# Retention's values: headed products in pairs of row tiles, and the first chunk's turned rows between the second chunk's pairs

## The reference

```python
V = jnp.einsum('bshd,hde->bshe', vh, Wh)
masked = scores * Dn[None, :, :, :]
A = jnp.maximum(jnp.abs(masked.sum(axis=0)), 1.0)
O = jnp.einsum('hst,bthe->bshe', A, V).reshape(b, s, dim)
mu = O.mean(axis=-1, keepdims=True)
var = O.var(axis=-1, keepdims=True)
Y = (O - mu) / jnp.sqrt(var + GN_EPS) * gn_gamma + gn_beta
W = jax.nn.relu(x @ wg_w)
return W * Y @ wo_w
```

## Time and profile before

| | |
|---|---|
| median of 3 runs | 1602.47 us (1602.07 to 1602.49) |
| the profiled execution's own time | 1602.21 us |
| its span in the profile | 1600.5 us |
| mean granted TensorE clock | 0.995 of full speed |
| TensorE (PE) busy | 1557.8 us, 97% of the span |
| VectorE (DVE) busy | 1192.6 us, 75% |
| ScalarE (ACT) busy | 1034.2 us, 65% |
| GpSimd (POOL) busy | 481.6 us, 30% |

### The profile page before, as it was taken

How to read it: one execution, slowest core, us unless ns; L and a number is a source line. 1 busy time by engine, 2 the same in 40 slices (tenths; PEclk the granted TensorE clock), 3 DMA queues, 4 the chain that set the end, 5 groups by cost and what they waited for, 6 DMA issues and landing times.

```text
span 1600.5 us, 28360 instructions
## 1 busy us (share of the span) xinstructions
PE 1557.8 (97%) x9554; PEld 1210.9 (76%) x9554; DVE 1192.6 (75%) x2455; ACT 1034.2 (65%) x2863; POOL 481.6 (30%) x516
## 2 busy tenths in 40 slices
PE   7989979999999999999999999999999999999998
PEld 6888756666776777777777777777777777777887
DVE  7668876766996888888888887777777777898322
ACT  4564437663568888778787787777777777874100
POOL 1000222224534434434334334334344344320000
PEclk9999989999999999999999999999999999999999
DMA  8631568986663232373333363121151221100001
GB/s 310 211 105 60 180 216 276 310 289 196 212 210 132 80 124 87 113 253 103 113 120 115 113 221 93 54 72 57 56 204 55 73 90 52 59 28 7 27 33 40
DMA packets 79849, 206.11 MB, mean 129 GB/s; under 512 B 7344, under 2 KB 27824, under 8 KB 74224
## 3 DMA queue, kind: packets, MB, share of 16 engines
q1 hardware_dynamic: 74048, 185.94, 34.0%
q0 software_dynamic: 5680, 18.62, 3.8%
HBM read 151.83 MB, written 52.69 MB: 128 GB/s over the span
## 4 chain that ended last, share of the span: by engine, by line
PE 79%; DVE 4%; ACT 1%; DMA 1%; POOL 1%; issue 1%; SPq 0%; POOLq 0%; ACTq 0%; DVEq 0%
PE bank L103 11%; PE bank L105 10%; PE bank L104 10%; PE bank L2682 10%; PE bank L2683 10%; PE bank L2744 7%; PE bank L2768 6%; PE bank L2733 5%; PE bank L1537 4%; PE bank L2754 3%; PE bank L1496 1%; DMA s_rows<-x_rows,t_tok 1%; POOL t_rs L2647 1%; ACT t_sc L2899 1%; PE bank L1526 1%
## 5 line engine op out<-in xcount | busy, mean ns | idle before, releaser
L2682 PE MATMUL bank<-t_half,t_xh 128*128 128x256 f16 (+1 forms) x1024 | 309.3, 326 | 0.0
L2683 PE MATMUL bank<-t_half,t_xh 128*128 128x256 f16 (+1 forms) x1024 | 306.0, 326 | 0.0
L2644 POOL TENSOR_SCALAR t_ve<-t_ss 128x4 f32<-128x4 f32 (+1 forms) x128 | 25.9, 202 | 563.8 <-DVE t_ss L2997 537.6
L2899 ACT ACTIVATE t_sc<-bank,t_mx 128x128 f32<-128x128 f32 x512 | 180.3, 381 | 15.9 <-DVE t_mx L3037 10.8
L2647 POOL TENSOR_TENSOR t_rs<-t_ve,t_mhalf 128x4 f32<-128x4 f32 (+1 forms) x128 | 172.3, 1346 | 10.7
L3001 DVE TENSOR_TENSOR t_hn<-bank,t_rs 128x256 f32<-128x256 f32 (+1 forms) x256 | 130.2, 551 | 59.8 <-POOL t_rs L2647 59.5
L2683 PEld LDWEIGHTS bank<-t_half,t_xh 128*128 128x128 f16 x1024 | 100.2, 98 | 66.0
L2682 PEld LDWEIGHTS bank<-t_half,t_xh 128*128 128x128 f16 x1024 | 100.3, 98 | 65.7 <-issue 0.5
L2937 ACT ACTIVATE t_y<-bank,smooth 128x128 bf16<-128x128 f32 x512 | 139.7, 402 | 2.3 <-DVE t_cq L1379 2.3
L2768 PE MATMUL bank<-t_wp,t_cq 128*128 128x512 f16 x512 | 130.7, 379 | 0.0
L2744 PE MATMUL bank<-t_hT 128*128 128x128 f32 x1024 | 126.2, 276 | 2.4 <-ACT t_hT L2926 2.0
(11 more groups left out here) (372 smaller groups left out, 3984.4 us busy)
## 6 DMA issues: line engine op xcount, KB each, us to landing
t_xh<-xq_scratch SPq DMA_DIRECT2D x64, 512.0 KB, 3.4
t_cr<-in_ctxT_dram SPq DMA_DIRECT2D x64, 256.0 KB, 2.6
t_half<-w_half SPq DMA_DIRECT2D x12, 1024.0 KB, 6.6
y_rows<-s_y SPq DMA_DIRECT2D x39, 256.0 KB
w_rows<-in_w_qkv_dram SPq DMA_DIRECT2D x8, 1024.0 KB
xq_scratch<-z_xs SPq DMA_DIRECT2D x16, 512.0 KB, 3.8
t_slot<-w_plain SPq DMA_DIRECT2D x4, 2048.0 KB, 8.9
t_raw<-in_w_proj_dram SPq DMA_DIRECT2D x4, 2048.0 KB, 10.4
```

Of the source, the lines that this page charges most:

```text
L2682: nc.tensor.matmul(out, rows[:, k, kind, :], w[0][:, k, a:b], start=k == 0, stop=False)
L2683: last = nc.tensor.matmul(out, rows[:, k, kind, :], w[1][:, k, a:b], start=False, stop=k == KT - 1)
L2899: last = nc.scalar.activation(sc[:, h, :], b3[4 + part][:, n, :], ACT.Exp, bias=mx[:, h:h + 1], accum_out=sm[:, h:h + 1])
```

## The change

In `Values` only. First, `headed` on TensorE runs over pairs of row tiles (0 and 1, then 2 and 3), and in a pair over the heads, with the two row tiles inside. Each head has its own wait for `uT`. For chunks 1 and 3 the waits for free banks are for both banks of a pair. Second, in step 1 TensorE runs the first pair of `headed(1)`, then `turned(0)`, then the second pair; ScalarE copies `o_sb(1)` of the first pair, then makes the four `yT(0)` (`turned_out`), then copies the second pair and takes the root, then makes the `z_hi(0)` (`turned_high`). VectorE passes no parts, and its program stays as it is.

```diff
--- before.py
+++ after.py
@@ -678,13 +678,19 @@
         self.st, self.mv = at("st", 157.25, [P, J, 6]), at("mv", 157.375, [P, J, 2])
         self.va, self.sd, self.rs = (at(n, 157.5 + i / 32, [P, J]) for i, n in enumerate(("va", "sd", "rs")))
 
-    def steps(self, attention, turned, projected):
+    def steps(self, attention, turned, projected, parts=None):
         for i in range(C + 2):
             if i < C:
                 attention[0](i)
-            if i == 1:
+            if i == 1 and parts:
+                attention[1](i, range(1))
+                parts[0](i - 1)
+                attention[1](i, range(1, 2))
+                parts[1](i - 1)
+            elif i == 1:
                 attention[1](i)
-            if 1 <= i <= C:
+                turned(i - 1)
+            elif 1 <= i <= C:
                 turned(i - 1)
             if i < C and i != 1:
                 attention[1](i)
@@ -733,20 +739,23 @@
                                             start=True, stop=True)
                 last.then_inc(self.u_ps, 1)
 
-        def headed(c):
+        def headed(c, pairs=range(2)):
             if c == 0:
                 pe.wait_ge(re.wh_in, 16)
                 pe.wait_ge(re.w_sb, C * KT)
-            pe.wait_ge(self.u_sb, c * KT + KT)
-            for j in range(J):
+            for pair in pairs:
+                js = range(2 * pair, 2 * pair + 2)
                 if c == 1:
-                    pe.wait_ge(self.o_in, j + 1)
+                    pe.wait_ge(self.o_in, js[-1] + 1)
                 if c >= 3:
-                    pe.wait_ge(self.x_in, (c - 3) * J + j + 1)
+                    pe.wait_ge(self.x_in, (c - 3) * J + js[-1] + 1)
                 for h in range(KT):
-                    last = nc.tensor.matmul(bank[4 + j][:, ramp(h)], self.uT[:, h, ramp(j)], re.wh[:, h, :],
-                                            start=True, stop=True)
-                last.then_inc(self.o_ps, 1)
+                    pe.wait_ge(self.u_sb, c * KT + h + 1)
+                    for j in js:
+                        last = nc.tensor.matmul(bank[4 + j][:, ramp(h)], self.uT[:, h, ramp(j)], re.wh[:, h, :],
+                                                start=True, stop=True)
+                        if h == KT - 1:
+                            last.then_inc(self.o_ps, 1)
 
         def turned(c):
             pe.wait_ge(self.y_n, c * J + J)
@@ -779,7 +788,7 @@
                 pe.wait_ge(self.x_in, (C - 1) * J + 1)
                 so.logits(pe, 0)
 
-        self.steps((scored, headed), turned, projected)
+        self.steps((scored, headed), turned, projected, (turned, lambda c: None))
 
     def scalar(self, act):
         nc, env = self.nc, self.env
@@ -792,22 +801,30 @@
                     act.wait_ge(self.o_ps, c * J)
                 nc.scalar.activation(self.uT[:, h, :], bank[h][:], ACT.Copy).then_inc(self.u_sb, 1)
 
-        def headed(c):
-            for j in range(J):
-                act.wait_ge(self.o_ps, c * J + j + 1)
-                if c:
-                    act.wait_ge(self.y_n, (c - 1) * J + j + 1)
-                nc.scalar.activation(self.o_sb[:, j, :], bank[4 + j][:], ACT.Copy).then_inc(self.o_in, 1)
-            act.wait_ge(self.eps_in, c + 1)
-            nc.scalar.activation(self.sd[:], self.va[:], ACT.Sqrt).then_inc(self.root, 1)
+        def headed(c, pairs=range(2)):
+            for pair in pairs:
+                for j in range(2 * pair, 2 * pair + 2):
+                    act.wait_ge(self.o_ps, c * J + j + 1)
+                    if c:
+                        act.wait_ge(self.y_n, (c - 1) * J + j + 1)
+                    nc.scalar.activation(self.o_sb[:, j, :], bank[4 + j][:], ACT.Copy).then_inc(self.o_in, 1)
+            if 1 in pairs:
+                act.wait_ge(self.eps_in, c + 1)
+                nc.scalar.activation(self.sd[:], self.va[:], ACT.Sqrt).then_inc(self.root, 1)
 
         def turned(c):
+            turned_out(c)
+            turned_high(c)
+
+        def turned_out(c):
             for f in range(KT):
                 act.wait_ge(self.t_ps, c * KT + f + 1)
                 if c:
                     act.wait_ge(self.z_in, (c - 1) * KT + f + 1)
                 nc.scalar.activation(self.yT[:, f, :], bank[f][:], ACT.Identity, scale=env.col("gamma", f),
                                      bias=env.col("beta", f)).then_inc(self.y_T, 1)
+
+        def turned_high(c):
             for f in range(KT):
                 act.wait_ge(self.z_in, c * KT + f + 1)
                 if c >= 2:
@@ -824,7 +841,7 @@
                 self.so.high(act, 1)
                 self.so.high(act, 2)
 
-        self.steps((scored, headed), turned, projected)
+        self.steps((scored, headed), turned, projected, (turned_out, turned_high))
 
     def vector(self, dve):
         nc, env, re, so = self.nc, self.env, self.re, self.so
```

## The result

The change makes the kernel slower by 0.28%: the median of 20 executions is 1607.53 us (1603.83 to 1613.12), against 1602.48 us (1600.64 to 1607.77) in 20 of before; the ratio is 1.0028, 95% interval 1.0022 to 1.0034, so 4.5 us (3.5 to 5.4); the two medians are 5.05 apart. The forecast was 1604.2 us and no change that a measurement can tell, the range ended at 1606.3. Two later comparisons of the same kernel gave 1.0034 (1.0022 to 1.0045) and 1.0024 (1.0014 to 1.0033). The mean granted clock of the 20 executions is 0.9905, with the change, and 0.9942 to 0.9945 before (three sets of 27 to 35 executions). Since the clock is either full or half, the time at 1.2 GHz is 2 x (1 - clock) x span: 31 us in an execution against 18. The span profiled is 1604.8 us (before 1600.5), the execution's own time 1606.53.

What follows compares the result with a forecast made beforehand. TensorE, busy 97% of the span, was taken to bound the kernel, with the start of `projected(0)` deciding. Chain +1.3 and clock +0.4 gave +1.7 us on 1602.47, so 1604.2 us, range 1602.3 to 1606.3.

Steps and rivals of the forecast that it cites:

- +1.3: Last statistics on VectorE start 1.3 us later, behind the fourth `o_sb(1)`; the delay passes on to `uT(2)`.
- What TensorE gained: TensorE reaches `scored(2)` 2.1 us sooner, but waits behind it; the hole grows from 1.24 to about 4.6 us.
- I take 0.4: Clock fall behind the hole ahead of `turned(1)`: 3.0 us at 1.2 GHz lose 1.5, of which 0.4 us is cost.
- the losses fall in `turned(1)` and `headed(2)`, which have 1.10 us to spare: Clock losses ahead of `projected(0)` are partly absorbed: 1.5 us lost costs 0.4, 3.6 us costs 2.5.
- At chunk 0 the same gain is worth nothing: `headed(0)` by pairs gains nothing, as `scored(1)` waits for the context load and stays at 100.18.
- A shift of the start of `projected(0)` therefore reaches the end one to one: Only two waits, 1.1 and 0.7 us, were read behind `projected(0)` up to 186 us, so its shift passes through whole.
- two waits behind `projected(0)`: In the trace before, TensorE has only waits of 1.1 and 0.7 us behind `projected(0)` up to 186 us.
- The delay without the clock: Rival, 17%: only the chain's +1.3 us, no clock loss, 1603.8 us.
- The gain that comes through: Rival, 7%: `scored(2)`, not `uT(2)`, holds `turned(1)`, so TensorE's 2.1 us pass; 1600.4 us.
- the wash: Rival, 8%: VectorE or ScalarE catch up; 1602.0 to 1602.7 us.
- The waits per head: Rival, 3%: 8 waits in `headed` at chunk 3 hold up weight loads, +0.8 us on top, 1605.0 us.
- The long low clock: Rival, 10%: clock stays at 1.2 GHz long after the hole ahead of `turned(1)`; +1.3 + 2.5 = +3.8, 1606.3 us.

Runs made afterwards that it cites:

- the filled kernel: The change plus 16 matmuls of no use on TensorE between `scored(2)` and `turned(1)`; 1.0006 to the kernel before.
- three kernels: `headed(0)` waits for all four `uT(0)`, in the change (1.0018), the change with the hole filled (1.0011), and pairs by head with altered ScalarE order (0.9989).
- the two shifted kernels: 8 matmuls of no use (1.8 us) ahead of `turned(2)`, in the change (1.0026) and in the kernel before (1.0008).
- The filled kernels: The change with 16 matmuls of no use ahead of `turned(1)`, 1.0006; the same with `headed(0)` waiting for all four `uT(0)`, 1.0011.
- a second pair of kernels: The change with `headed(0)` waiting for all four `uT(0)`, 1.0018; the same with 16 matmuls of no use ahead of `turned(1)`, 1.0011.

## Why the prediction was wrong

**The chain was right.** The starts that it gave up to `turned(1)` are in the profile: `headed(1)` 103.86 (103.86), `turned(0)` 105.70 (105.65), the second pair 107.45 (107.39), `scored(2)` 109.5 (109.65), the last `o_sb(1)` ending at 110.42 (110.36), `uT(2)` 117.2 (117.19), `turned(1)` 117.9 (117.91), the hole about 4.6 us (4.43). "+1.3" is 1.29 at `uT(2)` and 1.28 in the distance of the filled kernel. What TensorE gained did become a wait behind `scored(2)`.

**The step that failed is "I take 0.4", the price of the clock.** It should have been about 3.2 us (4.5 less 1.3). It was too small at the one place where the prediction looked, and left out two others.
- At the hole ahead of `turned(1)` it costs 0.2 to 1.5, 1.0 on the average of five profiles. The price was taken from one fall of 3.0 us, while the low stretch of the change's profile is 6.8 us long, 4.5 of them behind the restart. The 3.0 stopped at 500 us; the next five us of the kernel before (below) have 0.96, 0.4 us more. And "the losses fall in `turned(1)` and `headed(2)`, which have 1.10 us to spare" holds only in part: a slow `turned(1)` also slows `yT(1)`, which stands in ScalarE's full queue, and from `uT(2)` to `o_sb(2)` that queue took 7.17 us in place of 6.64. These 0.53 us had nothing to spare. The prediction had the longer case as a rival with 10%, at +3.8 in all.
- "At chunk 0 the same gain is worth nothing" counted only that `scored(1)` cannot start sooner. Starting `headed(0)` sooner widens the hole ahead of `scored(1)` from 0.88 to 2.01 us, and behind such a hole (1.7 to 2.3 us) `scored(1)` took 5.45 to 5.47 us in place of 3.84 in 3 of 8 profiles: 1.6 us each, 0.6 on average. With the hole at 1.13 us or less it did so in none of 6. The times do not bear out the 0.6: the wait that keeps this hole short was tried on three kernels, and they became 1.6 us faster, 0.8 slower and 0.5 slower.
- "A shift of the start of `projected(0)` therefore reaches the end one to one" holds for work, not for the clock. The barrier's idle 1.95 us are a place where the clock falls in some executions, for 2.4 us in the change's profile. Of the 5 unshifted profiles with the fall ahead of `turned(1)`, 4 have it; of the 7 unshifted ones without, 1. With the two shifted kernels it is 4 of 6 and 2 of 8. A link would fit the 1.6 us that are left of the 3.2 (4 in 5 less 1 in 7, by 2.4 us, is 1.6; by all fourteen 1.0), and the low time that went in the first of the two filled kernels. But it stands on few profiles, and what would link them isn't shown.

```profile
500.00:505.00 5.00, 5.00 (x34) 3.69 (x34) 2.67 (x6) 4.36 (x18) 0.66 (x1) 0.96 0.15 51
```

The filled kernels (1.0006 and 1.0011, low time 17 and 19) put the 3.2 us down to the clock; how it divides among the three places is an estimate from a few profiles.

The prediction also reads the earlier trace rows as two waits behind `projected(0)`. The first of them is the one ahead of it. Nothing hung on this: from the start of `projected(0)` to the barrier the delay went from 2.00 to 2.03 us.

**The rivals.** The delay without the clock is what the filled kernel is, 1.0006, and it takes work of no use to get there. The gain that comes through and the wash are out: `turned(1)` waited for `uT(2)`, which came 1.29 us late. All six profiles with a hole over 4 us in front of `turned(1)` show the clock fall there. The waits per head are out: at chunk 3, where the rival had them, the 16 matmuls of `headed` take 3.74 us in the change as before. The long low clock was the nearest, its sum (1606.3) 1.2 below the median, but as one mechanism at one place; the profiles show falls at three.

**The rule of the Trainium skill.** The Trainium skill, TensorE: Matmul & The Clock Gate, "HAM oscillation — how this bites in real kernels", says that long waits throttle the clock and that the next work starts cold. The traces agree: behind all six holes of over 4 us the granted clock was below 1.00, 0.66 to 0.89 from 118 to 128 us. The prediction weighed this only for the largest hole. The kernel before pays for such falls as well, as its 18 us of low time show; its executions run from 1600.64 to 1607.77 us, a spread that the first three, 0.4 us apart, did not tell.

## What to carry to other kernels

Price every hole in TensorE's work that a change widens, the ones that "cost nothing" too, by what the work behind it takes at the lower clock and by how often the clock falls behind such holes in the traces at hand, and compare the mean clocks of the executions as well as their times. Work that TensorE does sooner gains nothing while what it needs next stands in another engine's queue: there the order of that queue was the lever, worth 2.5 us in this stage and about 2 in the time.

## What the runs showed of the hardware

- A hole of 4.3 to 4.7 us ahead of `turned(1)` was followed by the 1.2 GHz level in six of six profiles. A hole of 1.7 to 2.3 us ahead of `scored(1)` was followed by it in three of eight, one of 1.13 us or less there in none of six. Behind the barrier's idle 1.95 us it came in six of fourteen, and cost 2.3 to 2.7 us.
- At the lower level 16 fp32 matmuls of 128 x 128 took 5.45 us in place of 3.84 when the fall came in their course, and 16 transposes 3.13 to 3.65 behind the long hole in place of 1.91 to 2.03.
- 3.6 us of matmuls whose result nobody reads, put into a hole of 4.4 us, gave the kernel about 3.5 us back (1.0028 to 1.0006), and 1.1 us in a second pair of kernels, whose intervals overlap (1.0018 to 1.0011).
- Transposes at the lower level hold up the engine that reads them: ScalarE's four `yT(1)` took 3.28 us in place of 2.81.
